# Attention projections and expert results on one Trainium2 core: bias fill, row adds and vector schedule moved

## The reference

```python
tok = xn.reshape(B, H * W // 16, 16)              # 16-wide tokens
q, k, v = split(tok @ qkv_w)
att = concat(branch(q8, k8, v8, rows), branch(q8, k8, v8, columns)) @ proj_w + proj_b
normed = (att - mean(att)) * rsqrt(var(att) + 1e-5) * ln_w + ln_b
attention = transpose(tok + normed, (0, 2, 1)).reshape(B, H, W)
experts = sum over 6 of 16 routed experts of weight * down(silu(gate(x)) * up(x)) + shared expert
```

## Time and profile before

| what | us |
|---|---|
| three runs, median | 450.07 |
| three runs, lowest and highest | 444.04, 453.33 |
| the profiled execution | 446.27 |
| its span | 444.5 |
| last add of a fetched group ends | 438.28 |

### The profile page before, as it was taken

The page is one execution under the profiler, slowest core; times in us unless marked ns, Lnnn a source line. Parts: engine busy times, 40 slices in busy tenths (PEclk is TensorE's granted clock), DMA queues, the critical chain, the costliest instruction groups (busy, mean ns, idle before and its releaser), DMA issues.

```text
span 444.5 us, 7377 instructions
## 1 busy us (share of the span) xinstructions
PE 398.3 (90%) x1990; PEld 307.4 (69%) x1990; DVE 359.7 (81%) x602; ACT 237.9 (54%) x664; POOL 232.8 (52%) x221
## 2 busy tenths in 40 slices
PE   7898999999999999998999999998899999999400
PEld 7687888889667777775776777766667777767200
DVE  3869895986999999999999999999985265677961
ACT  3754334327465577775677677764447744565200
POOL 3531067785777877771000003711777777768581
PEclk9898899999999999999999999999999999999855
DMA  6998522228366666686633334744557996665662
GB/s 179 345 411 359 200 76 102 75 97 280 129 196 200 198 203 206 200 247 182 193 110 97 99 100 122 206 134 127 152 163 215 251 274 188 175 171 163 166 177 81
DMA packets 55880, 80.56 MB, mean 181 GB/s; under 512 B 8481, under 2 KB 47265, under 8 KB 55585
## 3 DMA queue, kind: packets, MB, share of 16 engines
q1 hardware_dynamic: 42912, 50.91, 37.6%
q0 software_dynamic: 9216, 25.96, 19.4%
q10 hardware_dynamic: 3712, 3.21, 2.5%
HBM read 43.48 MB, written 36.57 MB: 180 GB/s over the span
## 4 chain that ended last, share of the span: by engine, by line
PE 59%; DVE 18%; issue 8%; POOL 4%; DMA 4%; SPq 2%; ACT 2%; POOLq 1%; DVEq 0%; ACTq 0%
PE gate L1047 21%; PE ps_y L1070 15%; PE ps_y L1063 4%; PE up L1037 4%; POOL xs_dram L624 3%; PE ps_y L998 3%; PE gate L976 2%; PE up L976 2%; PE misc L1097 2%; DVE qkv L1150 2%; DVE yacc L1701 2%; DVE prod L1150 2%; DVE inter_s L1619 2%; PE misc L938 2%; SPq L471 2%
## 5 line engine op out<-in xcount | busy, mean ns | idle before, releaser
L1047 PE MATMUL gate<-wrec,xgT 128*128 x444 | 150.8, 462 | 4.6 <-DVE inter_s L1619 3.5
L624 POOL DMA_INDIRECT xs_dram<-xrow,slot_i x96 | 109.4, 1139 | 48.8 <-issue 20.7
L1070 PE MATMUL ps_y<-wrec,interT 88*128 x444 | 114.2, 380 | 0.4 <-DVE interT L1633 0.3
L1047 PEld LDWEIGHTS gate<-wrec,xgT 128*128 128x128 f32 x444 | 75.6, 190 | 30.0 <-issue 6.0
L1070 PEld LDWEIGHTS ps_y<-wrec,interT 88*128 88x128 f32 x444 | 75.4, 190 | 7.0 <-issue 0.9
L1619 DVE SCALAR_TENSOR_TENSOR inter_s<-gate,xg,gate_s 128x176 f32<-128x176 f32 x111 | 43.7, 394 | 39.5 <-ACT gate_s L769 39.2
L650 POOL DMA_INDIRECT gat<-xs_dram,slot_e x50 | 54.9, 1098 | 34.0 <-DVE yacc L1701 20.0
L789 ACT ACTIVATE y_s<-ps_y 128x256 f32<-128x256 f32 x107 | 41.1, 384 | 52.1 <-PE up L1037 50.1
L769 ACT ACTIVATE gate_s<-gate 128x176 f32<-128x176 f32 x111 | 35.4, 319 | 57.4 <-PE ps_y L1063 55.1
L1063 PEld LDWEIGHTS ps_y<-ident,inter_s 128*88 128x88 f32 x222 | 26.4, 123 | 36.8 <-issue 19.8
L1063 PE MATMUL ps_y<-ident,inter_s 128*88 128x128 f32 x222 | 42.5, 273 | 4.0 <-ACT y_s L789 1.5
(11 more groups left out here) (222 smaller groups left out, 666.8 us busy)
## 6 DMA issues: line engine op xcount, KB each, us to landing
xg<-xs_dram SPq DMA_DIRECT2D x111, 136.0 KB, 2.5
xs_dram<-y_s SPq DMA_DIRECT2D x111, 128.0 KB, 2.0
wrec<-wexp SPq DMA_DIRECT2D x14, 608.0 KB, 14.0
xs_dram<-zrow SPq DMA_DIRECT2D x1, 2176.0 KB, 12.0
xn_dram<-xrow SPq DMA_DIRECT2D x8, 256.0 KB, 3.6
qkv<-xn_dram SPq DMA_DIRECT2D x8, 256.0 KB, 5.1
xs_dram<-xrow,slot_i POOLq DMA_INDIRECT x96, 2.9
wrec<-wexp SPq DMA_DIRECT2D x1, 1216.0 KB, 6.0
```

The costliest lines, as they stand in the source:

```text
L624: nc.gpsimd.indirect_dma_start(xs_dram[0:DONE[max(d for d in DONE if d <= c)] * P, :], bass.IndirectOffsetOnAxis(slot_i[:, o:o + 1], 0), x ...
L1047: last = nc.tensor.matmul(guA[t % 2][:, 0:2 * I], xgT[:, t % 2, k * P:(k + 1) * P], wrec[:, bass.ds(record + k * 2 * I, 2 * I)], start=(k ...
L1070: last = nc.tensor.matmul(ps_y[:, t % 2 * 2 * H:t % 2 * 2 * H + H], interT[:, t % 2, k * P:(k + 1) * P], wrec[0:HALF, bass.ds(record + KT ...
```

## The change

The bias of six of the eight projection pieces is written to psum by ACT (an `ACT.Copy` of 128x512) in the pass before the piece, and PE only adds its product. All of the projection work (transposes of the second half, weights, projections, `NORM_AT`) comes two passes earlier, the last attention copies one pass earlier. The rows `xn2` swap places with `Z`, are loaded eleven passes earlier (`XN_AT` 76, with waits for `attx_ok` 12 and `lepe_used` 3), and are added straight into `yacc` by four new instructions (`add_rows`, passes 84, 86, 88, 90) in place of four sums inside `normalise()`. `Z` is stored with columns outermost, so that the last sum of each block reads in order. `ADD_AT` has one group a pass and lists 30 groups in place of 24.

```diff
-           ..., 84: ((3, 0), (3, 1)), 85: ((3, 2), (3, 3))}
+           ..., 83: ((3, 0), (3, 1)), 84: ((3, 2), (3, 3))}
-                 87: (8, 9), 88: (10, 11), 89: (12, 13), 90: (14, 15)}
+                 85: (8, 9), 86: (10, 11), 87: (12, 13), 88: (14, 15)}
-XN_AT = 87
+XN_AT = 76
+XT_AT = {84: 0, 86: 1, 88: 2, 90: 3}
-PROJECTIONS_AT = {91 + j: (j,) for j in range(8)}
-PROJECTION_WEIGHTS_AT = range(85, 89)
-NORM_AT = 100
+PROJECTIONS_AT = {89 + j: (j,) for j in range(8)}
+PROJECTION_WEIGHTS_AT = range(83, 87)
+NORM_AT = 98
-for _n, _t in enumerate((74, 74, 75, 75, 79, 80, 82, 84, 86, 87, 89, 91, 92, 93, 94, 95, 97, 98, 99, 100, 101, 102, 104, 105)):
+for _n, _t in enumerate((74, 75, 76, 77, 79, 80, 82, 83, 85, 86, 87, 88, 89, 91, 92, 93, 94, 95, 96, 97, 98, 99, 101, 102,
+                          105, 106, 107, 108, 109, 110)):
-        Z = qkv[:, 4096:8192]
-        xn2 = qkv[:, 8192:12288]
+        xn2 = qkv[:, 4096:8192]
+        Z = qkv[:, 8192:12288]
-                    sp.wait_ge(attx_ok, 16)
+                    sp.wait_ge(attx_ok, 12)
+                    sp.wait_ge(lepe_used, 3)
+                for j in PROJECTIONS_AT.get(t + 1, ()):
+                    if j < 2:
+                        continue
+                    act.wait_ge(z_sb, j - 1)
+                    nc.scalar.activation(misc[j % 2][:, :].rearrange("p (t c) -> p t c", c=C),
+                                         row[:, R_PB:R_PB + C].unsqueeze(1).to_broadcast([P, 32, C]), ACT.Copy).then_inc(bias_ok, 1)
-                    pe.wait_ge(z_sb, j - 1)
-                nc.tensor.matmul(misc[j % 2][:, :], ones[:, :], prow[:, :].unsqueeze(1).to_broadcast([2, 4, P]),
-                                 start=True, stop=False, skip_group_check=True)
+                    pe.wait_ge(bias_ok, j - 1)
+                else:
+                    nc.tensor.matmul(misc[j % 2][:, :], ones[:, :], prow[:, :].unsqueeze(1).to_broadcast([2, 4, P]),
+                                     start=True, stop=False, skip_group_check=True)
-                nc.vector.tensor_tensor(Zt[:, 32 * j:32 * j + 32, :], misc[j % 2][:, :].rearrange("p (t c) -> p t c", c=C),
-                                        row[:, R_LNW:R_LNW + C].unsqueeze(1).to_broadcast([P, 32, C]), ALU.mult).then_inc(z_sb, 1)
+                nc.vector.tensor_tensor(Zc[:, :, 32 * j:32 * j + 32], misc[j % 2][:, :].rearrange("p (t c) -> p c t", c=C),
+                                        row[:, R_LNW:R_LNW + C].unsqueeze(2).to_broadcast([P, C, 32]), ALU.mult).then_inc(z_sb, 1)
-                    tt(part, part, dev.unsqueeze(2).to_broadcast([P, 2 * P, TILES]), ALU.mult)
-                    yield
-                    tt(part, part, xt[:, :, some], ALU.add)
+                    tt(part, part, dev.unsqueeze(1).to_broadcast([P, TILES, 2 * P]), ALU.mult)
                     yield
                     settle()
+                    dve.wait_ge(xt_ok, NBLK)
                     dve.wait_ge(added, sums.value())
-                    nc.vector.tensor_tensor(acc, acc, part.rearrange("p t c -> p c t"), ALU.add).then_inc(norm_ok, 1)
+                    nc.vector.tensor_tensor(acc, acc, part, ALU.add).then_inc(norm_ok, 1)
+            def add_rows(b):
+                acc = yacc[:, b * 1024:(b + 1) * 1024].rearrange("p (c t) -> p c t", c=TILES)
+                dve.wait_ge(xn_in, 16 * 8)
+                dve.wait_ge(added, sums.value())
+                nc.vector.tensor_tensor(acc, acc, xt[:, TILES * b:TILES * b + TILES, :], ALU.add).then_inc(xt_ok, 1)
+                lines.add()
+                if t in XT_AT:
+                    add_rows(XT_AT[t])
                 if t >= NORM_AT:
-                    next(late)
+                    next(late, None)
```

More of the change, by code:

```diff
@@ L118 @@
 ATTX_AT = {40: ((0, 0),), 41: ((0, 1),), 42: ((0, 2),), 43: ((0, 3),), 44: ((1, 0),), 45: ((1, 1),), 46: ((1, 2),), 47: ((1, 3),),
-           65: ((2, 0),), 66: ((2, 1),), 67: ((2, 2),), 68: ((2, 3),), 84: ((3, 0), (3, 1)), 85: ((3, 2), (3, 3))}
+           65: ((2, 0),), 66: ((2, 1),), 67: ((2, 2),), 68: ((2, 3),), 83: ((3, 0), (3, 1)), 84: ((3, 2), (3, 3))}
 TRANSPOSES_AT = {50: (0,), 51: (1,), 52: (2,), 53: (3,), 54: (4,), 55: (5,), 56: (6,), 57: (7,),
-                 87: (8, 9), 88: (10, 11), 89: (12, 13), 90: (14, 15)}
+                 85: (8, 9), 86: (10, 11), 87: (12, 13), 88: (14, 15)}
 LEPE_FROM = {1: 18, 2: 30, 3: 58}
@@ L363, in build @@
         lepe_ok, lepe_used = sem("lepe_ok"), sem("lepe_used")
+        bias_ok, xt_ok = sem("bias_ok"), sem("xt_ok")
         row = cst[:, C_ROW:CONSTS]
@@ L1643, in tile_result @@
                 nc.vector.tensor_copy(y_s[:, t % YRING, :], ps_y[:, t % 2 * 2 * H:t % 2 * 2 * H + H]).then_inc(y_sb, 1)
-            Zt = Z.rearrange("p (t c) -> p t c", c=C)
+            Zc = Z.rearrange("p (c t) -> p c t", c=C)
+            xt = xn2.rearrange("p (t c) -> p c t", c=C)
             var = mx[:, :, :].rearrange("p h t -> p (h t)")
@@ L1672, in normalise @@
                 dve.wait_ge(z_sb, 8)
-                dve.wait_ge(xn_in, 16 * 8)
-                xt = xn2.rearrange("p (t c) -> p t c", c=C)
                 for b in range(NBLK):
-                    some = slice(TILES * b, TILES * b + TILES)
-                    part = Zt[:, :, some]
+                    part = Zc[:, TILES * b:TILES * b + TILES, :]
                     acc = yacc[:, b * 1024:(b + 1) * 1024].rearrange("p (c t) -> p c t", c=TILES)
-                    tt(part, part, dev.unsqueeze(2).to_broadcast([P, 2 * P, TILES]), ALU.mult)
-                    yield
-                    tt(part, part, xt[:, :, some], ALU.add)
+                    tt(part, part, dev.unsqueeze(1).to_broadcast([P, TILES, 2 * P]), ALU.mult)
                     yield
                     settle()
+                    dve.wait_ge(xt_ok, NBLK)
                     dve.wait_ge(added, sums.value())
-                    nc.vector.tensor_tensor(acc, acc, part.rearrange("p t c -> p c t"), ALU.add).then_inc(norm_ok, 1)
+                    nc.vector.tensor_tensor(acc, acc, part, ALU.add).then_inc(norm_ok, 1)
                     parts.add()
                     yield
-            sums, parts = Tally(), Tally()
+            sums, parts, lines = Tally(), Tally(), Tally()
+            def add_rows(b):
[4 more added lines that the diff above has]
+                lines.add()
             def add_results(n):
@@ L1698, in add_results @@
                     dve.wait_ge(added, sums.value())
+                if lines.value():
+                    dve.wait_ge(xt_ok, lines.value())
                 if parts.value():
```

## The result

The changed kernel took 456.87 us (median of four runs) against 449.33 for the kernel before (four runs): ratio 1.0167, 95% interval 1.0099 to 1.0236. Its median lies above the range, which ended at 455.0. The profiled execution took 456.82 us, its span is 455.0. Both kernels were then measured again twice, with more runs: the changed kernel 449.51 and 449.28 us (12 runs each), ratios to the kernel before 0.9989 (0.9949 to 1.0030) and 1.0026 (0.9980 to 1.0072). A ratio leaves out executions more than 1.5% above the fastest of their kernel, which fall in a slower state; a median holds them all. These ratios compare with all executions of the kernel before in the same session (29 and 23); beside 12 executions of it in the same rounds, with medians 446.74 and 446.25, the changed kernel's are 2.8 and 3.0 us higher.

The account below looks back on a forecast made before the run. POOL's fetches were taken to bound the end: breaks -6.0 + 0.6 and lengthening +3.3 gave -2.1 us, with PE's saved 2.55 us not counted. From the median 450.07 that made 448.0 us, range 441.0 to 455.0.

Parts of the forecast that it names:

- the breaks at 418 and 421: Pauses of 3.25 and 1.01 us between POOL's fetches in the kernel before; forecast to go.
- The fill's waits: ACT's bias fills in six passes: done in time, the wait for DVE's scaling normally not late, cost to PE nothing.
- Bounds: After the projections, time saved on PE counts only if POOL's fetches come earlier; POOL's queue nearly closed from 327.85 us.
- start of group 8: First fetch of the 71 steps from 327.85 us; no shift forecast, as POOL's own queue holds the early groups.
- extension of groups 8 to 41: Fetch time over 0.95 us, lengthened by DVE sums: 15.4 us against 12.1, so +3.3.
- breaks: POOL's three pauses, 6.0 us together, go; some 0.6 is left before group 24.
- last landing and add: The tail behind POOL's last fetch, its landing and DVE's last add: stays as before.
- Early sums one a pass: DVE's early adds spread over passes: cost 0, between a gain of 0.5 and a loss of 0.5 us.
- a PE wait of 3 us or more: Sign that the forecast is right: PE waits this long around the square root.
- The second: Rival: POOL's queue, passes 84 to 104, becomes the clock and is lengthened more; +6.1 us, 456.2; chance 0.22.
- a last fetch after 435: Sign for the slower rival: POOL's last fetch begins after 435 us; the forecast had it near 433.
- The first (rows free for POOL): Rival: the four row adds do not hold up POOL; 5.0 us come off, -7.1, 443.0 us; chance 0.28.

Follow-up runs that it names:

- the two sooner versions: Changed kernel, table of before from group 8 on, first eight adds in passes 69 to 79: ratio 0.9798; the other also adds rows through psum: 0.9848.

## Why the prediction was wrong

**The size.** The range ended at 455.0 and the first median was 456.87. The step of the prediction that put the number outside is one it never wrote down: it took the time ahead of the first edit as the same in both kernels, a term of zero, and 9.2 us lie there in the profile. By the repeats the changed kernel stands 0.1% below to 0.3% above the kernel before, at 449.5 and 449.3. That is near the forecast of 448.0 but no success of it: the forecast was 0.5% faster than its base of 450.07, and beside the kernel before in the same rounds the changed one is 2.8 and 3.0 us slower. The time to tile 74 varies by 10 us; I read 444.04 to 453.33 in the three runs as noise around one number and asked no view where it came from.

**Mechanism: right in part.** That a fetch is held by a DVE instruction with two SBUF operands (by 0.12 us less than that instruction still had to run), that PE falls back to the pace of the fetches (group 23 ends 5.2 us later than before, forecast six; tile 103 comes 7.2 later), that the breaks at 418 and 421 go, that fills last 0.60 (measured 0.595 to 0.602) and that their gain does not show in the end: each is in the profile after. The fill's waits, which I put at zero for PE, are 0.4 us before piece 7's matmuls at 384.37; ACT itself waits 6.5 us in all for DVE's scaling in five of the six fills, where I expected it to be normally in time.

**Bounds: wrong in part.** That POOL's queue and not PE bounds the kernel is true only of its last part. The chain that ended last in the kernel before runs mostly through PE up to 409.66, then through DVE's sums, and through POOL only from 427.33:

```profile
408.25 1.19 PE gate L1047 x4
...
427.33 0.95 POOL gat L650
```

So PE's time counts there, and the fill alone in that kernel takes 3.8 us off the stretch. In the changed kernel POOL waits 4.05 us for PE's tile 98 before group 24.

**The sum**, term by term, for the stretch, in the first pair of profiles:

| term | forecast | measured |
|---|---|---|
| start of group 8 | 0 | +3.4 |
| extension of groups 8 to 41 | +3.3 | 9.8 against 12.1: -2.3 |
| breaks | -5.4 | 6.15 against 6.0: +0.1 |
| last landing and add | 0 | +1.0 |
| sum | -2.1 | +2.3 (of unrounded terms) |

The extension came out 5.6 us under the forecast and the breaks 5.5 over it. That the time from the first fetch of group 8 to the last fetch, 105.1 us, met the forecast is luck.

*Early sums one a pass* is the first term that failed. I costed it at 0 and said that POOL's queue holds those groups anyway; I had looked at PE and DVE only. An early sum moved by a pass moves the attention sums behind it and with them the moments at which a fetch can start: the one at 333.22 took 2.01. Groups 4 to 7 are lengthened by 7.1 us in place of 2.6. The kernel before with that edit alone shows 8.0, but its stretch does not grow (133.0), and in the changed kernel the term is worth at most 1.8 us at the end.

*The breaks* are the second, and the step that decides. I closed all three and left 0.6 before group 24, with PE and POOL both about six late there. POOL's queue was 5.2 us late at the end of group 23 (407.0 - 313.95 against 392.6 - 304.74), and group 24, which waits for tile 98's store, 7.5: DVE's waits in `add_results` hold the variance and with it ACT and PE for longer than they hold POOL. I had named this chain, with a PE wait of 3 us or more, and left it out of the sum. What the runs show in its place: adds placed before their fetch has landed stop PE for 4.6 us, its clock halves meanwhile, and the new passes of groups 7 to 23 alone cost 5.9 us of stretch; I had costed those adds at 1.0, all of it POOL's. Putting groups 24 to 29 in front of the last gates then made a second break, before group 36, that I had not looked for (2.1 us in two of the three profiles of the changed kernel, 0.1 in the third); alone, that part costs 2.8 us.

*Extension* was overpriced: the four fetches beside the row adds took 0.97, 0.79, 0.77 and 0.84 us more than 0.95, together 3.4 and not 5.0, and the block sums of 1.22 us hit fewer fetches since POOL was idle twice.

**The rivals.** The second had the right sign and the right place, POOL's queue in passes 84 to 104, and its sign of a last fetch after 435 came true (445.49, or 436.3 without the 9.2 us ahead of tile 74), but it had the wrong means: the mean step of the fetches from group 8 on was 105.1 / 71 = 1.48 us, what I expected and under the 1.51 where it was to decide. The loss came from where the queue starts and where it stops. The first (rows free for POOL) is refuted by 345.91. As for the Trainium skill, page "SBUF — State Buffer", section "Who interferes with whom": its rule that a DVE instruction with two SBUF inputs contends with a GpSimd instruction that reads SBUF agrees with the traces here, with 1.92 us at 345.91, and so does its other half, one SBUF input and no hold-up, with 0.95 us at 392.15; its inferred remark that `tensor_tensor` does not hold up descriptor generation does not agree with the fetch of 1.92 us beside the first row add.

## What to carry to other kernels

An add that waits for a transfer is a wait for all that stands behind it on its engine, so place it by when the transfer lands, a pass or two later than it could be, and never in front of a step that another engine waits for; the same change with its old table of passes is 1.5% faster than the kernel before (0.9795 to 0.9896), with the new one it is not faster at all. Before pricing an edit at zero, lay it against every queue that it can hold up, not only against the engine that looks critical. And when runs of one kernel differ by 2%, find the mark in the trace behind which they agree, and compare kernels from there.

## What the runs showed of the hardware beyond what was expected

POOL's indirect sends, the last of which the tiles from 39 on wait for, meet DVE's instructions differently from execution to execution of the same code: in the seventeen profiles what they took over 0.95 each was 17.6 to 26.6 us in all, and tile 74 came between 303.7 and 314.1 (the two sooner versions have four more adds ahead of it). PE's wait for the last of them was 1.56 to 8.20 us. Behind it the granted clock, as the mean of 200 to 230 us, was 1.00 in the five with waits up to 1.97, 0.94 or 0.89 in the eight with 2.2 to 5.5, and 0.83 in the four with 8.1 to 8.2, in both kernels alike. That is why 6.2 us more of waiting make 9 us of delay: PE stands still and then works in part at 1.2 GHz. What makes one execution fall into this and another not was not found. The same happens later in the changed kernel, where the adds make PE wait 4.6 us: the clock falls to 0.50 in that wait, and the gate of a tile then takes 2.55 us in place of 1.35 (2.56 in the first profile).
